# The opening of an RWKV block kernel: VectorE takes the weight remainders, the first maximum and K(0,1) move ahead

## The reference, cut to what matters

```python
# x: 4 sequences x 1024 tokens x 512 channels, float32
xk = x_prev + (x - x_prev) * tmk        # the same for xv, xr: mixing with the token before
k, v, r = xk @ Wk.T + bk, xv @ Wv.T + bv, xr @ Wr.T + br
wkv = _wkv_scan(k, v, time_decay, time_first)   # recurrence over time, with a running maximum
x = layernorm(x + (sigmoid(r) * wkv) @ Wo.T + bo)
# then a mixture of 8 experts, the best one for each token, and a second layernorm
x = layernorm(x + gate * (x @ W[expert].T + b[expert]))
```

## Time and profile before

| | |
|---|---|
| median of 3 runs | 662.0 us |
| the profiled execution: its time, its span | 662.49 us, 660.7 us |
| mean granted clock of TensorE in it | 0.963 |
| PE busy | 600.1 us (91%) |
| DVE busy | 519.8 us (79%) |
| ACT busy | 389.4 us (59%) |
| POOL busy | 279.5 us (42%) |

### The profile page before, as it was taken

How to read it: one execution, slowest core, us unless ns; L and a number is a source line. 1 busy time by engine, 2 the same in 40 slices (tenths; PEclk the granted TensorE clock), 3 DMA queues, 4 the chain that set the end, 5 groups by cost and what they waited for, 6 DMA issues and landing times. The chain is left out here.

```text
span 660.7 us, 8344 instructions
## 1 busy us (share of the span) xinstructions
PE 600.1 (91%) x2328; PEld 400.9 (61%) x2329; DVE 519.8 (79%) x826; ACT 389.4 (59%) x727; POOL 279.5 (42%) x213
## 2 busy tenths in 40 slices
PE   0666788999999999999999999999999999999991
PEld 0455576677668668767767866775566454454440
DVE  7958899999999999899999899888833666444441
ACT  3446466566756757647746766561345667667662
POOL 5743553551552453544445155211023555555521
PEclk9779889999999999999999999989979999999996
DMA  8030010022104104103102211635566565656520
GB/s 306 14 127 1 0 64 0 0 67 94 32 18 142 33 0 137 54 0 111 64 16 93 67 33 37 218 145 185 192 216 156 155 235 177 217 178 209 195 103 0
DMA packets 36563, 67.61 MB, mean 102 GB/s; under 512 B 8560, under 2 KB 8560, under 8 KB 36532
## 3 DMA queue, kind: packets, MB, share of 16 engines
q1 hardware_dynamic: 30292, 48.29, 22.3%
q0 software_dynamic: 6240, 18.94, 9.2%
HBM read 50.17 MB, written 18.88 MB: 105 GB/s over the span
## 5 line engine op out<-in xcount | busy, mean ns | idle before, releaser
L1053 POOL TENSOR_TENSOR mixed<-unsplit,mixed 128x1024 fp32r<-128x1024 f32 x44 | 104.4, 2393 | 133.7 <-ACT mixed L748 133.7
L680 PE MATMUL y_ps<-w_e,xgT 128*128 x312 | 140.0, 592 | 0.0
L499 PE MATMUL kb<-mixed,w_kvr 128*128 128x512 f32 x384 | 99.0, 409 | 25.5 <-DVE mixed L1396 17.0
L499 PE MATMUL vb<-mixed,w_kvr 128*128 128x512 f32 x384 | 101.8, 416 | 13.3 <-DVE evn L1234 7.6
L499 PE MATMUL rb<-mixed,w_kvr 128*128 128x512 f32 x384 | 102.4, 417 | 5.1 <-DVE ee L1248 3.8
L499 PEld LDWEIGHTS kb<-mixed,w_kvr 128*128 128x128 f32 x384 | 74.2, 197 | 44.1 <-issue 16.7
L517 PE MATMUL y_ps<-w_o,rw 128*128 128x512 f32 x224 | 100.7, 592 | 0.0
L499 PEld LDWEIGHTS vb<-mixed,w_kvr 128*128 128x128 f32 x384 | 73.9, 197 | 34.4 <-DVE evn L1234 10.4
L680 PEld LDWEIGHTS y_ps<-w_e,xgT 128*128 128x128 f32 x312 | 56.4, 190 | 56.9 <-issue 56.9
L499 PEld LDWEIGHTS rb<-mixed,w_kvr 128*128 128x128 f32 x384 | 74.1, 195 | 27.1 <-issue 6.2
L1185 DVE SCALAR_TENSOR_TENSOR unsplit<-diff,vec,xb 128x512 f32<-128x512 f32 x96 | 74.2, 834 | 8.0 <-PE kb L499 6.0
(11 more groups left out here) (216 smaller groups left out, 920.6 us busy)
## 6 DMA issues: line engine op xcount, KB each, us to landing
bias<-b_experts SPq DMA_DIRECT2D x39, 256.0 KB, 3.6
w_e<-w_experts SPq DMA_DIRECT2D x8, 1024.0 KB, 7.8
rows<-x SPq DMA_DIRECT2D x28, 256.0 KB, 2.6
x_rows<-rows SPq DMA_DIRECT2D x28, 256.0 KB, 2.1
xb<-xT SPq DMA_DIRECT2D x4, 1026.0 KB, 5.4
xb<-xT SPq DMA_DIRECT2D x3, 1024.0 KB, 5.1
w_raw<-w_square SPq DMA_DIRECT2D x2, 1024.0 KB, 10.4
xb<-xT SPq DMA_DIRECT2D x2, 512.0 KB, 5.5
```

Source lines behind the costliest of these rows:

```text
L499: mm = pe.matmul(bank, w_kvr[m][:, a, h, o:o + P], mixed[m][:, bb, h, :], start=(k == 0), stop=(k == 3 * CH - 1))
L680: mm = pe.matmul(y_ps[:, n % 2, :], xgT[n % 3][:, c, :], w_e[:, bass.ds(e, 1), c, :].rearrange("p u o -> p (u o)"), start=(c == 0), stop=( ...
L1053: pool.tensor_tensor(mixed[m][:, LO, 2 * hp:2 * hp + 2, :], unsplit[m][:, LO, 2 * hp:2 * hp + 2, :], mixed[m][:, HI, 2 * hp:2 * hp + 2, :] ...
```

## The change

DVE subtracts all weight remainders, in four new calls `weight_lo`, and POOL none. On DVE the first maximum and distance stand directly behind the mixing of V, and the input remainders of V and the bias remainder come later. On PE K(0,1) stands ahead of V(0,0). On ACT the high part of the first half of K's input stands between the two halves of K's weights, and R's weights ahead of V's input.

```diff
@@ PE
             project(0, K, 0)
+            project(0, K, 1)
             project(0, V, 0)
-            project(0, K, 1)
@@ ACT
             for hp in range(2):
                 act.wait_ge(w_k_loaded[hp], 16)
                 act.activation(w_kvr[K][:, HI, 2 * hp:2 * hp + 2], ...).then_inc(w_hi, 1)
-            mix_hi(0, K, 0)
-            mix_hi(0, K, 1)
+                mix_hi(0, K, hp)
             (bo's high part)
-            act.wait_ge(w_loaded[V], 16)
-            act.activation(w_kvr[V][:, HI], w_raw[V][:], ACT.Copy).then_inc(w_hi, 1)
+            for m in (V, R):
+                act.wait_ge(w_loaded[m], 16)
+                act.activation(w_kvr[m][:, HI], w_raw[m][:], ACT.Copy).then_inc(w_hi, 1)
             mix_hi(0, V, 0)
             mix_hi(0, V, 1)
-            act.wait_ge(w_loaded[R], 16)
-            act.activation(w_kvr[R][:, HI], w_raw[R][:], ACT.Copy).then_inc(w_hi, 1)
@@ POOL
-            for hp in range(2):
-                pool.wait_ge(w_hi, hp + 1)
-                half = slice(2 * hp, 2 * hp + 2)
-                pool.tensor_tensor(w_kvr[K][:, LO, half], ..., ALU.subtract).then_inc(w_lo, 1)
-            for m in (V, R):
-                pool.wait_ge(w_hi, m + 2)
-                pool.tensor_tensor(w_kvr[m][:, LO], ..., ALU.subtract).then_inc(w_lo, 1)
@@ DVE
+            def weight_lo(m, c0, c1, n):
+                dve.wait_ge(w_hi, n)
+                dve.tensor_tensor(w_kvr[m][:, LO, c0:c1], w_raw[m][:, c0:c1], w_kvr[m][:, HI, c0:c1].bitcast(F32),
+                                  ALU.subtract).then_inc(w_lo, 1)
             first_lo(K, 0)
+            weight_lo(K, 0, 2, 1)
+            weight_lo(K, 2, 4, 2)
             first_lo(K, 1)
+            mix_matrix(0, V, 0)
+            mix_matrix(0, V, 1)
+            running_max(0, 0)
+            distance(0, 0)
+            first_lo(V, 0)
+            first_lo(V, 1)
+            weight_lo(V, 0, CH, 3)
             (bo's remainder)
-            mix_matrix(0, V, 0)
-            mix_matrix(0, V, 1)
-            first_lo(V, 0)
-            first_lo(V, 1)
             mix_matrix(0, R, 0)
             mix_matrix(0, R, 1)
+            weight_lo(R, 0, CH, 4)
             dve.wait_ge(bias_moved, 32)
             dve.wait_ge(zero_stored, 16)
-            running_max(0, 0)
-            distance(0, 0)
```

More of the change, by code:

```diff
@@ L1112, in _ @@
             pool.tensor_copy(ones[:], filled[:]).then_inc(route_const, 1)
-            for hp in range(2):
-                pool.wait_ge(w_hi, hp + 1)
-                half = slice(2 * hp, 2 * hp + 2)
-                pool.tensor_tensor(w_kvr[K][:, LO, half], w_raw[K][:, half], w_kvr[K][:, HI, half].bitcast(F32), ALU.subtract).then_inc(w_lo, 1)
-            for m in (V, R):
-                pool.wait_ge(w_hi, m + 2)
-                pool.tensor_tensor(w_kvr[m][:, LO], w_raw[m][:], w_kvr[m][:, HI].bitcast(F32), ALU.subtract).then_inc(w_lo, 1)
             walk(pool, step, pool.Fori)
```

## The result

The changed kernel takes 653.7 us (median of 4 runs, 651.95 to 653.92) against 661.88 us of the kernel before beside it: a ratio of 0.9865, 95% interval [0.9846, 0.9884]. That is 8.2 us less; the forecast was 8.0 (654.0). The profiled execution is the shortest of the four, 651.95 us with a span of 649.8 us, so its trace shows 10.9 us less than the trace before.

What follows compares the result with a forecast made beforehand. The prediction took PE to bound the body and DVE, stretched by POOL, the opening. R(0,0) moving from 46.39 to 38.4 gave 8.0 us: 662.49 to 654.5 profiled, 654.0 for the median, range 652.0 to 658.5.

Steps and rivals of the forecast that it cites:

- DVE is the opening's chain, and 12.8 us of it are exclusion: Opening: DVE's two-SBUF-input instructions are stretched by POOL's subtractions, as both cannot run together; DVE loses 12.8 us.
- Rival 3: Opening: DVE's stretches belong to the place, not POOL, and stay on top of 7.2 us added; 665.4 us, chance 0.05.
- The new timeline: Opening, part by part: first scan at 20.2, `weigh_now` done 7.4 us earlier, R(0,0) at 38.4, 8.0 us earlier.
- The doubtful spot: R's weight remainder on DVE at 30.1, when POOL asks 0.06 us earlier: DVE keeps on until 32.6, POOL ends at 37.3.
- 19.24: Time before the change when POOL came 0.1 us before a mixing instruction's end, yet DVE went on until about 22.5.
- 12.42 and 26.80: Times before the change when POOL was already waiting as DVE finished, and DVE's next instruction lost; cited for rival 1.
- V(0,1) at 4.4 us: PE, behind a pause of 3.2 us: V(0,1) takes 4.4 us, not 2.95, and ends at 38.4, which decides R(0,0).
- rival 2: PE: V(0,1) runs at the fast pace, 2.95 us, until 37.0; gain 9.1, 652.9 us, chance 0.14.
- Everything behind R(0,0) merely moves: Rest of the kernel: gate, denominator and next chunks hang on R(0,0), so its 8.0 us shift stands until the end.
- K(0,1) ahead of V(0,0): PE in the opening: K(0,1) fills time in which V(0,0) has no weights, until 27.0.
- rival 1: R's weight remainder at 30.1: POOL wins the turn, R(0,0) starts at 41.0; gain 5.4, 656.6 us, chance 0.25.

Runs made afterwards that it cites:

- remainders_only: The kernel before with only the four POOL weight-remainder subtractions moved to DVE, in the old order: 658.28 us, ratio 0.9934.
- order_only: The changed kernel with the weight remainders back on POOL, the new order of DVE, PE and ACT kept: 659.81 us, ratio 0.9963.
- again: The changed kernel measured a second time, unchanged: 653.63 us, ratio 0.986.
- pe_back: The changed kernel with V(0,0) ahead of K(0,1) on PE again: 652.99 us, ratio 0.9854.
- hold: The changed kernel with two more 128x2048 subtractions (results unused) directly ahead of R's weight remainder on DVE: 658.2 us, a single execution.
- start_early_bias_late: The changed kernel with ACT's start values ahead of V's inputs and the bias remainder moved behind the second distance: 652.12 us, ratio 0.9841.
- start_early: The changed kernel with ACT's three start values written ahead of V's inputs: 652.87 us, ratio 0.9846.
- fill_start_early_bias_late: The changed kernel with start values early, bias remainder late and 11 unused matmuls in PE's pause before V(0,1): 650.91 us, ratio 0.9813.

## Why the prediction was right

- **DVE is the opening's chain, and 12.8 us of it are exclusion.** Right, and shown: **remainders_only** has the same order and no stretch. Rival 3 (the place) is out.
- **The new timeline.** K(0,0) at 14.0 (13.46 measured), first scan 20.2 released by ACT (19.57, by ACT), K(0,1) 22.3 (21.64), V(0,0) straight behind it, `weigh_now` done at 34.0 (32.82). Of the 1.2 us at the end 0.5 are x landing earlier in that execution (first difference at 5.83, before 6.32), 0.4 the two large remainders (taken as 2.4, they take 2.28 and the next instruction starts 2.20 behind them), and 0.3 that the smaller subtractions follow each other at 1.13 to 1.14, not 1.19.
- **The doubtful spot.** DVE kept its turn at 29.22, though POOL had asked first, and so it did in the seven other traces with the same two instructions there. But the reason given was weak, and that it came out so is in part luck: the prediction took 19.24 as the same situation in form and set 12.42 and 26.80 against it, and overlooked 10.10, where POOL also came out of idleness just before the end of a DVE instruction, 0.07 us ahead of the next one, and won. In **order_only** POOL won even in the form of 19.24.
- **V(0,1) at 4.4 us.** The term that varies: 3.02 in the first trace (rival 2), 4.60 in the second. In the second, which lies near the median, R(0,0) is at 37.4 where 38.4 was forecast.
- **8.0 forecast, 8.2 measured: partly luck.** R(0,0) came 10.26 us earlier in one trace and 9.02 in the other, more than the 7 to 8.6 of the forecast in both, because DVE's chain was forecast 1.1 to 1.2 us too slow and, in the first, V(0,1) ran at the fast pace. The span of **again** is 9.0 shorter than that of the trace before, but its time only 8.6 (662.49 to 653.91), and the trace before was itself 0.6 above the median of the runs beside the change (661.88). Against the 662.48 of the next runs of before the same kernel gains 8.85. The mechanism is right; the last digit of the agreement is not earned.
- **Everything behind R(0,0) merely moves.** Right to 0.5 us over the blocks (10.26 to 9.80); between the last distance and the first expert's addition the two traces of the changed kernel are 1.1 and 0.3 us shorter than the one before, which the forecast did not have.
- **What was wrong without showing in the sum.** K(0,1) ahead of V(0,0) was taken as filling free time; it is worth nothing (**pe_back**): it leaves a pause before V(0,1), behind which V(0,1) takes 4.60 in **again**, where it takes 2.88 in **pe_back**. For R's weights ahead on ACT the prediction gave a cost (nothing) and no gain; undone together with the rest of ACT's order they cost 3.5 us.

The Trainium skill's rule on the shared pair ("SBUF — State Buffer", section "SBUF: two separate sides") holds in its first half: one engine has the pair and the other stands. Its second half, that the one which starts first gets it, would have given rival 1, 656.6; POOL started 0.07 us ahead in the changed kernel and waited 2.2 us all the same, though at 10.10 before the change it started 0.07 us ahead and got it. By itself this half decides nothing here.

## What to carry to other kernels

An engine that is busy all the time may be waiting inside its instructions: compare each instruction's length with the same form elsewhere before believing the busy share, and look for the other engine's instruction that ends just before. Moving work onto the engine that seems to be the bottleneck can then shorten it, 6.9 us of added work against 12.8 us of exclusion here. A serial opening is paid in full at the end, so each wait on its chain is worth about its length, and once the chain is short, the pace of the first matmuls behind a pause is the next term.

## What the runs showed of the hardware that was not expected

- GpSimd was kept out while VectorE had three subtractions with two SBUF inputs ready: 8.96 us for an instruction of 2.4 (**hold**). VectorE's instructions with a PSUM input ran beside GpSimd's at their usual 0.73 and 1.26 us. In other places GpSimd got the first turn with a lead of the same size.
- The same 12 matmuls took 3.02 us behind a pause of 2.71 us and 4.60 behind one of 3.67, but 5.49 behind one of 3.08 (**start_early_bias_late**), 4.60 and 3.03 behind two of 2.10 (K(0,1) in **start_early** and **fill_start_early_bias_late**), and 4.34 to 5.46 for K(0,0) after 13 to 17 us of nothing. The length of the pause alone does not give the pace.
- The record of the clock does not always go with the pace: from 13 to 19 us it shows 1.00 in **again**, while K(0,0) takes 5.46 us there, and 1.00 as well from 33.0 to 37.4 in the first trace, where V(0,1) takes 3.02.
